# One step of mixing, half of a normalisation and two reciprocal roots moved in a fused two-layer network

## The reference

```python
# layer 0
x = x + attention(ln_c(x))     # windows of 8x8 queries, 12x12 keys, 6 heads of 16, relative positions
t = tokens(x)
t = t + ffn(ln_t(t))           # fp8e5 operands, fp16 sums, hidden 384, relu
x = image(t)
# layer 1
x = x + cluster(ln_c(x))       # see below
t = tokens(x)
t = t + ffn(ln_t(t))

# cluster: per quadrant of 128x128 and head of 24 channels
sim  = sigmoid(beta + alpha * l2norm(centres) @ l2norm(features))
sim  = sim * (one-hot of the best of 4 centres)
agg  = (sim @ value + value_centres) / (sum(sim) + 1)
out  = conv1x1(agg at each point, weighted by sim)
```

## Time and profile before

| | |
|---|---|
| median of 3 runs | 9184.56 us (9182.27 to 9190.45) |
| the profiled execution | 9189.38 us; span of its instructions 9187.4 us |
| mean granted clock of TensorE | 0.907 |
| PE busy | 7725.7 us (84%), 172050 matmuls |
| PEld busy | 6181.7 us (67%) |
| DVE busy | 7147.5 us (78%), 23940 instructions |
| ACT busy | 4849.8 us (53%) |
| POOL busy | 2499.9 us (27%) |
| DMA | 502.56 MB, mean 55 GB/s |

### The profile page before, as it was taken

One profiled execution on the slowest core, in us unless ns is written; L12 is line 12 of the kernel. 1 busy time (PEld: TensorE's weight loads), 2 busy tenths in 40 slices (PEclk: granted clock), 3 DMA queues, 4 the chain that ended last, 5 costly groups with the idle time before them and its releaser, 6 DMA issues.

```text
span 9187.4 us, 436110 instructions
## 1 busy us (share of the span) xinstructions
PE 7725.7 (84%) x172050; PEld 6181.7 (67%) x172050; DVE 7147.5 (78%) x23940; ACT 4849.8 (53%) x9750; POOL 2499.9 (27%) x4860
## 2 busy tenths in 40 slices
PE   6999999988888888888888888888888888887665
PEld 4777777776767666766766666766766666765443
DVE  3777777778888888887888878887888888887666
ACT  2555545545555555555555555555555555555445
POOL 1333332333223232232232222222232222232000
PEclk8999999999999999999999999998999999998556
DMA  2111111112222122222222222222222222221111
GB/s 59 47 43 44 51 47 48 50 52 52 61 56 60 55 54 59 55 56 56 58 54 59 55 54 58 56 56 55 60 54 59 55 54 59 55 57 51 58 57 59
DMA packets 193442, 502.56 MB, mean 55 GB/s; under 512 B 33508, under 2 KB 67108, under 8 KB 191468
## 3 DMA queue, kind: packets, MB, share of 16 engines
q1 hardware_dynamic: 191692, 476.75, 19.1%
HBM read 228.84 MB, written 169.93 MB: 43 GB/s over the span
## 4 chain that ended last, share of the span: by engine, by line
PE 52%; DVE 29%; issue 10%; ACT 6%; DVEq 1%; DMA 1%; SPq 0%; ACTq 0%; POOL 0%; POOLq 0%
PE scores_x L701 10%; PE flipped L723 6%; PE bank L605 4%; PE pv L751 3%; DVE maxes L1572 3%; PE bank L964 3%; PE bank L671 3%; PE misc L614 3%; DVE z L1687 2%; PE pv L745 2%; PE bank L991 2%; PE scores_x L641 2%; DVE shifted L1580 2%; PE bank L678 2%; DVE bn L1663 2%
## 5 line engine op out<-in xcount | busy, mean ns | idle before, releaser
L2022 POOL TENSOR_TENSOR vrest<-vstage,vmask 96x384 f32<-96x384 f32 x512 | 431.5, 843 | 4943.1 <-ACT vstage L1202 4943.0
L1572 DVE TENSOR_REDUCE maxes<-scores_x 128x6 f32<-128x864 f32 x1024 | 1078.9, 1054 | 727.0 <-PE scores_x L701 643.2
L701 PE MATMUL scores_x<-keys,queries 64*64 64x144 f32 x24576 | 1084.5, 310 | 552.6 <-DVE shifted L1580 541.2
L701 PEld LDWEIGHTS scores_x<-keys,queries 64*64 64x64 f32 x24576 | 788.6, 142 | 767.2 <-issue 715.5
L1239 ACT ACTIVATE probs<-flipped 128x384 f32<-128x384 f32 x1024 | 500.3, 489 | 1216.9 <-PE flipped L723 1214.7
L1580 DVE TENSOR_TENSOR shifted<-scores_x,maxes 128x768 f32<-128x768 f32 x1024 | 970.7, 948 | 0.8
L660 PE MATMUL bank<-xt,wq 97*32 97x64 f32 x24576 | 868.8, 223 | 93.9 <-issue 59.7
L663 PE MATMUL bank<-xn,wq 97*32 97x64 f32 x24576 | 889.4, 223 | 53.5 <-issue 53.1
L660 PEld LDWEIGHTS bank<-xt,wq 97*32 97x32 f32 x24576 | 740.8, 111 | 282.1 <-issue 195.2
L1190 ACT ACTIVATE queries<-bank 128x512 f32<-128x512 f32 x768 | 459.6, 598 | 881.3 <-PE bank L663 881.3
L723 PE MATMUL flipped<-ident,shifted 128*128 128x128 f32 x6144 | 902.4, 286 | 0.0
(11 more groups left out here) (189 smaller groups left out, 17432.4 us busy)
## 6 DMA issues: line engine op xcount, KB each, us to landing
keys<-kst SPq DMA_DIRECT2D x768, 99.0 KB
x_in<-x_dram SPq DMA_DIRECT2D x130, 396.0 KB
xn_kept<-xn SPq DMA_DIRECT2D x128, 388.0 KB, 3.8
later<-xn_kept SPq DMA_DIRECT2D x128, 388.0 KB, 3.4
x_tok<-tok_dram SPq DMA_DIRECT2D x128, 384.0 KB, 3.4
x_kept<-x SPq DMA_DIRECT2D x128, 384.0 KB, 2.3
later<-x_kept SPq DMA_DIRECT2D x128, 384.0 KB, 3.7
out_dram<-later SPq DMA_DIRECT2D x128, 384.0 KB, 2.4
```

Source lines behind the costliest of these rows:

```text
L701: last = mm(score[e][64 * j:64 * j + 64, g * NKEY:(g + 1) * NKEY], queries[64 * e:64 * e + 64, g, w, :], keys[64 * e:64 * e + 64, g, :, WS ...
L1572: V.tensor_reduce(maxes[:, p % 2, :, :], sc, AX.X, ALU.max).then_inc(max_ready.sem, 1)
```

## The change

Nothing is computed in another way. Pieces are moved.

- `mix` on PE goes from the tail into step 5, behind `pool`, and its DVE half from the tail into step 6. `spread` of strip n+1 in step 6 now waits for it, and `flip_heads(0)` stands ahead of `spread`.
- The second half's `ffn_stats` goes from the tail into step 0 of the next strip, its root into step 1 and its application (`ffn_apply`, new) into step 2. `flip_z` of that half goes from step 0 to step 2.
- That root is taken together with stream C's root (`rsqrt_c` is no longer called in the strips), and the root of A's input normalisation together with stream B's lengths, in chains of 12 and 44 columns. `squares_sum` goes from step 3 to step 4.
- The first block of values is no longer made in the tail in `fill`, but behind the next strip's first scores, in `work`; the second block goes to `fill`, behind the scores of step 1. `variance` on PE is done whole in step 3.
- VectorE's loops over strips are unrolled; the loop over quadrants 3 to 6 stays, and those of the late drains. The drains take the length root behind `mix`.

```diff
...
@@ -708,7 +710,7 @@
                     if p == 0:
-                        pe.wait_ge(v_stored.sem, v_stored.at(n, 1 + e))
+                        pe.wait_ge(v_stored.sem, v_stored.at(n, 3 + e))
                     else:
@@ -784,13 +786,17 @@
                     flip_z(n - 1, 0)
-                make_values(n, 1, work)
+                make_values(n, 0, work)
                 for p in range(TILES):
...
                         scores(p + 1)
+                    if p == 0:
+                        if on.c3:
+                            pe.wait_ge(hc_evac.sem, hc_evac.at(n - 1, 6))
+                        make_values(n, 1, fill)
 
                     if p == 0 and ahead:
-                        pe.wait_ge(v_stored.sem, v_stored.at(n, 4))
+                        pe.wait_ge(v_stored.sem, v_stored.at(n, 2))
                         mean(n + 1, 0)
@@ -802,7 +808,8 @@
                     if p == 3 and ahead:
-                        variance(n + 1, 2, on)
+                        for c in range(3):
+                            variance(n + 1, c, on)
                     if p == 4:
@@ -817,10 +824,12 @@
                     if p == 6:
+                        flip_heads(0)
+                        if on.c1:
+                            pe.wait_ge(mixed.sem, mixed.at(n, 2))
                         if ahead:
...
                             spread(n + 1, 1)
-                        flip_heads(0)
                     if p == 7:
@@ -832,21 +841,18 @@
                     if p == 0:
-                        if b1:
-                            flip_z(n - 1, 1)
                         if on.c3:
...
                         if b1:
-                            pe.wait_ge(zt_ready.sem, zt_ready.at(n - 1, 2))
+                            pe.wait_ge(zt_ready.sem, zt_ready.at(n - 1, 1))
                         flip_features(n, 0, k % 2)
-                    if p == 2 and ahead:
-                        if b1:
-                            pe.wait_ge(zt_ready.sem, zt_ready.at(n - 1, 2))
-                        variance(n + 1, 0, on)
-                        variance(n + 1, 1, on)
+                    if p == 2 and b1:
+                        if on.b:
+                            pe.wait_ge(ft_ready.sem, ft_ready.at(n, 2))
+                        flip_z(n - 1, 1)
                     if p == 3 and on.c2:
@@ -859,6 +865,10 @@
                             pool(n - 2)
+                        if on.c1:
+                            pe.wait_ge(v_stored.sem, v_stored.at(n, 8))
+                            mix(n, 0)
+                            mix(n, 1)
                     if b1 and p in (1, 2, 3):
@@ -877,12 +887,6 @@
                 weigh(TILES - 1)
-                if on.c1:
-                    for u in range(2):
-                        if ahead:
-                            pe.wait_ge(normed.sem, normed.at(n + 1, 2 + u))
-                        pe.wait_ge(v_stored.sem, v_stored.at(n, 8))
-                        mix(n, u)
                 if ahead:
@@ -890,17 +894,11 @@
                     make_queries(n + 1, 2)
-                    if on.c2:
-                        pe.wait_ge(hc_evac.sem, hc_evac.at(n, 5))
-                    make_main(n + 1, 0, fill)
                     make_queries(n + 1, 3)
...
                     make_queries(n + 1, 5)
-                    if on.c2:
-                        pe.wait_ge(hc_evac.sem, hc_evac.at(n, 6))
-                    make_rest(n + 1, 0, fill)
                 if on.b:
...
@@ -1216,8 +1213,10 @@
                     store_z(n - 1, 0)
-                store_values(n, 1, work)
+                store_values(n, 0, work)
                 for p in range(TILES):
+                    if p == 0:
+                        store_values(n, 1, fill)
                     if p == 1 and ahead:
@@ -1242,8 +1241,6 @@
                     if p == 0:
-                        if b1:
-                            store_z(n - 1, 1)
                         if on.c3:
...
@@ -1294,14 +1292,13 @@
                     store_queries(n + 1, 2)
-                    store_main(n + 1, 0, fill)
                     store_queries(n + 1, 3)
                     store_queries(n + 1, 4)
-                    store_queries(n + 1, 5)
-                    store_rest(n + 1, 0, fill)
                 if on.c2:
...
                     quantise_c(n, 5)
+                if ahead:
+                    store_queries(n + 1, 5)
 
...
@@ -1581,14 +1579,19 @@
                                     ALU.subtract).then_inc(s_shifted.sem, 1)
-                    if p == 0 and on.c2:
-                        stats_c(n, 1 - par)
+                    if p == 0:
+                        if on.c2:
+                            stats_c(n, 1 - par)
+                        if b1:
+                            ffn_stats(n - 1, 1)
                     if ahead and p in (1, 2):
...
                             centre_x(n + 1, 1)
-                    if p == 1 and on.c2:
-                        rsqrt_c(n)
+                    if p == 1 and b1:
+                        ffn_normalise(n - 1, 1, False, on.c2)
+                    if p == 2 and b1:
+                        ffn_apply(n - 1, 1)
                     if b1 and p in (3, 4, 5):
@@ -1601,21 +1604,36 @@
                             normalise_c(n, 1 - par)
+                    if not ahead and p == 4 and on.b:
+                        squares_sum(n, 0)
+                        squares_sum(n, 1)
+                        lengths(n)
                     if ahead and p == 4:
...
                         dve.wait_ge(newton_x.sem, newton_x.at(n + 1, 1))
-                        rsqrt_seed(rs_a_chain, newton_x, VT, 12)
-                        third_order(rs_a_chain, n + 1, VT, 12, newton_x, 2)
-                    if p == 4 and on.b:
-                        lengths(n)
+                        if on.b:
+                            squares_sum(n, 0)
+                            squares_sum(n, 1)
+                            lengths(n)
+                        at, parts, cols = (0, 128, 44) if on.b else (32, VT, 12)
+                        rsqrt_seed(rs_b_chain, newton_x, parts, cols, at)
+                        third_order(rs_b_chain, n + 1, parts, cols, newton_x, 2, at)
                     if p == 5:
                         if ahead:
-                            second_order(rs_a_chain, n + 1, VT, 12, newton_x, 6,
-                                         [(0, 12, rs_y[0:VT, 0:12], rstd_x)])
+                            at, parts, cols = (0, 128, 44) if on.b else (32, VT, 12)
+                            finals = [(32 - at, 12, rs_x[0:parts, :], rstd_x)]
+                            if on.b:
+                                finals += [(0, 32, rs_b_chain[3][:, 0:32], newton_n)]
+                            second_order(rs_b_chain, n + 1, parts, cols, newton_x, 6, finals, at)
+                        elif on.b:
+                            lone_root(n)
                         if on.b:
...
                     if p == 6:
+                        if on.c1:
+                            mix(n, 0, par)
+                            mix(n, 1, par)
                         if b1:
@@ -1635,9 +1653,6 @@
                             hidden_c(n, 3)
-                if on.c1:
-                    mix(n, 0, par)
-                    mix(n, 1, par)
                 if b1:
@@ -1645,14 +1660,13 @@
                 ffn_normalise(n, 0, b1)
+                ffn_apply(n, 0)
                 if on.c2:
...
                 residual(1)
-                ffn_stats(n, 1)
-                ffn_normalise(n, 1, False)
                 if on.b:
...
@@ -1679,7 +1696,13 @@
                     finals += [(4, TILES, mr[:, :, 1], newton_c)]
+                if with_c:
+                    cols = 4 + TILES
+                    finals += [(4, TILES, rs_c_chain[3][:, :], rstd_z)]
                 rsqrt(rs_a_chain, n, 128, cols, newton_f, base + 1, finals, at)
+
+            def ffn_apply(n, u):
+                at = (4 + TILES) * u
                 dve.wait_ge(rstd_f.sem, rstd_f.at(n, u + 1))
...
@@ -1746,24 +1772,26 @@
                               [:, :, C:C + EM]).then_inc(dots_ready.sem, 1)
+
+            def squares_sum(n, u):
                 V.tensor_reduce(norm2[:, 16 * u:16 * u + 16],
...
                 dve.wait_ge(norm2_ready.sem, norm2_ready.at(n, 2))
-                V.tensor_scalar(rs_b_chain[0][:, :], norm2[:, :], 1e-24, None, ALU.max
+                V.tensor_scalar(rs_b_chain[0][:, 0:32], norm2[:, :], 1e-24, None, ALU.max
                                 ).then_inc(norm2_ready.sem, 1)
                 dve.wait_ge(norm2_ready.sem, norm2_ready.at(n, 3))
-                rsqrt_seed(rs_b_chain, newton_n, 128, TILES * E1)
-                third_order(rs_b_chain, n, 128, TILES * E1, newton_n, 1)
+
+            def lone_root(n):
+                rsqrt(rs_b_chain, n, 128, TILES * E1, newton_d, 0,
+                      [(0, TILES * E1, rs_b_chain[3][:, 0:32], newton_n)])
 
             def cosine(n):
```

(35 more changed lines are left out.)

34 lines of the change are left out of this document (23 added, 11 removed).

## The result

The changed kernel takes 9052.54 us (median of 4 runs, 9045.06 to 9089.65) beside 9183.42 (4 runs, 9181.35 to 9190.45). The ratio is 0.987, with a 95% interval of 0.985 to 0.988: 131 us faster, where the forecast was 430, and outside the range. The profiled execution took 9053.59 us, its span is 9051.6, and its mean granted clock is 0.899, so lower than the 0.907 of before.

A forecast was written before the change was run, and what follows sets the result against it. Both engines were taken to wait in turn at the border between strips. Pieces sum to 61.4 us, with copies and clock 63.9 against 68.3; 93 strips gain 409, A and B 40, drains lose 20: median 8755, range 8600 to 8980.

The forecast's parts named there:

- c to e: From scores(2) to scores(5): 15.59 us a strip becomes 16.0, with `flip_z` added at 0.4 and `variance` moved for nothing.
- k: Tail from the last `weigh` to the next scores(0): 14.37 us becomes 10.45, with TensorE's own way put at 10.3.
- h to j: From scores(7) to the last `weigh` done: first part rises to 5.1 us, the others stay at 3.93 and 2.08.
- Piece a: From scores(0) to scores(1): 7.88 us falls to 3.35 as the second half's normalisation and the loop's end leave VectorE's way.
- b: From scores(1) to scores(2): 7.06 us becomes 7.05, the second values block adding about 1.7 and the better clock returning it.
- g: From scores(6) to scores(7): 5.02 us becomes 6.5, since `mix` on PE adds 1.56.
- straight code of VectorE: Rival: fetching stalls unrolled VectorE 2.2 us each time; two stalls a strip eat the gain, three give 9390; chance 0.06.
- Piece h: From scores(7) to the third `spread`: 4.22 us becomes 5.1, as VectorE's wait for `mix` makes the maxima 1.4 late.
- The copies: GpSimd's copies slow VectorE's statistics in steps 0 and 1 and `normalise(1)`: 1.0 us a strip, bounds 0 and 2.5.
- The clock: TensorE's remaining clock loss from short waits at the gather and in two pieces: 1.5 us a strip, bounds 0 and about 3.
- The base: Three-stream strip time before the change: 68.55 us less 0.25 for the edges, 68.3.
- A alone: Stage of 18 strips with only stream A: 0 gained, between -20 and 20, shorter steps offsetting the loop's end.

The follow-up runs named there:

- e11: The kernel before with VectorE's strip loops unrolled and nothing else; 9062.33 us, ratio to before 0.987.
- e5: The changed kernel with VectorE's strips in loops again, nothing else changed; 9192.18 us, ratio to before 1.001.
- e1: The changed kernel with the joined `variance` block of step 3 split into three groups in the same step; 8892.36 us, ratio to before 0.968.
- e12: The changed kernel with `flip_z` of the second half ahead of `weigh` in step 2, not behind the scores for step 4; 8901.66 us, ratio to before 0.969.
- e8: The changed kernel with three repairs: `variance` apart, a values block back between the queries, `flip_z` ahead of `weigh` in step 2; 8644.67 us, ratio to before 0.942.
- e4: The changed kernel with the keys' DMAs bringing one of 16 rows per head, so its keys are wrong; 8809.85 us, one run.
- e6: The changed kernel with `mix` back in the tail on PE and VectorE; 9005.54 us, ratio to before 0.983.
- e2: The kernel before with the first two `variance` blocks moved from step 2 to step 3, joined with the third; 9249.18 us, ratio to before 1.008.

## Why the prediction was wrong

The sign was right and the gain three times too large. The sign rests on the smallest part: the unrolling alone gives the measured time (e11), and the moves, which had three quarters of the forecast gain, gave nothing net as placed. The strip has 65.52 for a sum of 61.4: c to e are 2.0 too long and k 2.7, and h to j are 1.0 too short. Step by step:

- *Piece a (3.35), b (7.05), g (6.5), the loop's end (1.1 a strip)* held, or nearly: 3.73, 7.03, 6.40, and 125 to 140 us in all by e5 and e11, which is 1.4 a strip by the traces of e11. The straight code of VectorE starved nothing: with the loops back it is slower, not faster.
- *Piece h (5.1)* was too dear: h to j take 10.15 for the forecast 11.1. VectorE's wait for `mix` is there (199.4 us), and TensorE is not held up by it. *The copies (1.0)* do not show either: the addition of 128 x 4, which took up to 1.17 us before, takes at most 0.34 after, and a and b are as forecast without them.
- *Pieces c to e (16.0) failed: "`variance` moves between two steps of this stretch, which is nothing".* They take 17.98. The count of matmuls is unchanged, but joined they lower the clock: 1.4 a strip and 160 us in all (e1), where in the earlier trace rows I had tied the fall to long idle time. "`flip_z` comes in; I set it at 0.4" is the second part: it waits 0.67 for ScalarE's copy of z, and by e12 that placement costs 151 us with what it does to the clock.
- *Piece k (10.45) failed: "PE's own way is as long ... 10.3".* VectorE did its part nearly as forecast: `simw` is done 10.1 after the last `weigh`, for a forecast of 9.8. TensorE took 13.19. Taking 2.0 off for the values was plain subtraction, but without them idle time rose from 1.28 to 2.70 and low clock from 0.43 to 2.43, so the wait that ends last there is TensorE's own. That the values had been a pause in which instructions could come is my reading and not shown. With a block of values back k is 12.6, which is 10.3 + 2.0 and a little.
- *The clock (1.5, bounds 0 and about 3)* was argued from the one long wait. It came to 7.81 us a strip at 1.2 GHz, which at half speed is some 3.9 lost, above my bound. The sign of being wrong that I had named, "a clock as now with short gaps", is what came. But the reading that I had given to it, "that short waits suffice to lower it", is not what the runs show: with the wait of 0.65 left and the block apart the fall goes (e1), and with the wait gone and the block whole it is rarer but stays (e12).
- *The base (68.3)* was too high: "less 0.25 for the edges" is wrong. The five strips with an edge take 82 us where the other 88 take 67.6, which is 0.8 a strip over 93, and the strips without one took 67.72. So some 0.6 a strip, 54 us of the 409, was never there to be gained.
- *A alone (0, between -20 and 20)* lost 84: its low clock went from 58 to 202 us. With the three repairs the stage takes 959. *A and B (40)* gave 7, *the drains (20 slower)* cost 8.

e8, which keeps every move but these three placements, has 61.82, near the sum of 61.4. This agreement is in part luck: its c to e are 16.6 for 16.0, its h to j 10.1 for 11.1, and its first block of values stands in k and not in b. The prediction counted VectorE's work with care and took TensorE's side as fixed blocks that can be put anywhere.

The Trainium skill, "TensorE: Matmul & The Clock Gate", Terms, was used for the size of a loss; its half of the time below full clock fits e (3.10 low, 1.43 gained by e1). It was the number of falls, not their price, that I had wrong. The same page (Why this matters for your kernels) ties the fall to long idle gaps between matmuls; here it fell behind a wait of 0.64 us and 24 one-column matmuls; the measurement differs, and it decides.

What stays open: the mechanism of TensorE's stops in the queries. Their times fall together with the instruction packets, and the keys' DMAs lengthen them (e4), but 2.14 us of idle time is left without those DMAs. Nor is it shown what lowers the clock in k: it is low for 2.43 us in the kernel after, and for 0.52 and 0.59 in e4 and e6, though the idle time there is nearly the same (2.70, 2.14, 2.54).

## What to carry to other kernels

An edit that only reorders work on the bound engine is not free: look at what stands next to what. Here small matmuls gathered into one block, and worse behind a short wait, halved the clock of what followed, and taking other work out from between dense small matmuls lengthened TensorE's stops. And the worth of a move depends on where its pieces land: the same move was worth 0 as first placed, 165 us with its flips put elsewhere, and 225 with the other losses gone too. So test parts again once the largest loss is gone.

## What the runs showed of the hardware

- The clock fell to 1.2 GHz in a stretch in which TensorE was 100% busy by the profile, behind 24 matmuls with one moving column each and a wait of 0.64 us, in 59 of 85 strips. With the 24 in three groups and the same wait it fell in 1 (e1), without the wait in 50 (e12), and in the kernel before in none with groups of 16 and 8 and in 30 with the 24 joined (e2).
- The end of a VectorE loop body costs 2 us or more (83.2 us in 39 waits in the kernel before, 108.0 us in 37 waits in e5), and unrolling it saved 125 to 140 us of this kernel (e11, e5). By the Trainium skill, "Runtime: NRT & Kernel Launch", Instruction fetch mechanics, a taken branch to a page that is not loaded has to fetch it first; no run here shows whether that is what the 2 us are.
- In 13.2 us with some 410 matmuls TensorE stood still for 2.7 us with no releaser; half of the stops over 0.5 us end 1.37 to 1.61 us after an instruction packet.
